# Cross-attention with keys projected instead of queries, raw context attended in row tiles, and inputs laid out by the host

## What is computed

```python
# attention: query = layernorm(x), key = value = ctx (B=32, S=64, D=128), H=8
q = jnp.einsum('bsd,hdk->bhsk', query, Wq)
k = jnp.einsum('btd,hdk->bhtk', key, Wk)
v = jnp.einsum('btd,hdv->bhtv', value, Wv)
A = jnp.einsum('bhsk,bhtk->bhst', q, k)
A = m * A + (1.0 - m) * MASK_VALUE
A = jax.nn.softmax(A, axis=-1)
o = jnp.einsum('bhst,bhtv->bshv', A, v).reshape(...)
x1 = _layernorm(value + o @ Wo, gamma[0], beta[0])
x2 = x + _layernorm(x1 + relu(x1 @ W1 + b1) @ W2 + b2, gamma[1], beta[1])
# experts, on m = layernorm(x2): route to 4 of 16 (groups first), plus 2 shared
out = x2 + sum_e combine[:, e] * ((silu(m @ gate_e) * (m @ up_e)) @ down_e) + shared
```

## Time and profile before

| | |
|---|---|
| time, median of 3 runs | 350.35 us (350.18 to 351.27) |
| profiled execution | 350.7 us, its span 348.3 us |
| busy shares | PE 90%, PEld 73%, DVE 76%, ACT 52%, POOL 48% |
| granted TensorE clock, mean | 0.982 |
| instructions | 5536 |
| first keys or queries matmul | 16.12 us |
| first scores of c = 0, 1, 2, 3 | 23.06, 52.75, 86.36, 121.06 us |

### The profile page before, as it was taken

How to read it: one execution, slowest core, us unless ns; L and a number is a source line. 1 busy time by engine, 2 the same in 40 slices (tenths; PEclk the granted TensorE clock), 3 DMA queues, 4 the chain that set the end, 5 groups by cost and what they waited for, 6 DMA issues and landing times.

```text
span 348.3 us, 5536 instructions
## 1 busy us (share of the span) xinstructions
PE 312.4 (90%) x1683; PEld 254.7 (73%) x1683; DVE 263.7 (76%) x597; ACT 181.5 (52%) x338; POOL 168.9 (48%) x166
## 2 busy tenths in 40 slices
PE   3999899999999998986979799998989898989893
PEld 3979789798979896763858577776767676768662
DVE  2718426947994798898897956968888897969895
ACT  2564663476547653744528245555555645555541
POOL 3006413635563545267743468555655646464530
PEclk9999999999999999998998899999999999999998
DMA  8995000000000000004000065232333332333104
GB/s 240 347 272 191 3 0 3 0 0 2 3 1 0 2 0 2 2 2 128 0 0 1 2 176 194 92 107 104 120 120 120 120 105 89 112 116 120 60 0 122
DMA packets 18775, 26.81 MB, mean 77 GB/s; under 512 B 1330, under 2 KB 13124, under 8 KB 18628
## 3 DMA queue, kind: packets, MB, share of 16 engines
q1 hardware_dynamic: 16676, 25.52, 22.4%
q10 hardware_dynamic: 2080, 1.05, 1.0%
HBM read 25.38 MB, written 1.18 MB: 76 GB/s over the span
## 4 chain that ended last, share of the span: by engine, by line
PE 42%; DVE 22%; issue 15%; ACT 8%; POOL 8%; DMA 1%; DVEq 1%; POOLq 0%; ACTq 0%
PE bank L1223 8%; PE bank L1138 7%; PE bank L1201 7%; PE bank L1140 6%; PE bank L1139 6%; POOL wT L456 6%; DVE wT L1054 5%; DVE wT L1071 3%; ACT wT L682 3%; DVE cen L787 3%; PE bank L1250 2%; PE bank L1280 2%; DVE sc_m L830 1%; ACT prob_T L563 1%; DMA wqk_in<-in_L_xattn_Wq 1%
## 5 line engine op out<-in xcount | busy, mean ns | idle before, releaser
L1138 PE MATMUL bank<-mT_hi,we_hi 128*128 128x512 f32 x128 | 52.2, 408 | 3.1 <-DVE ctx_all L850 1.7
L1140 PE MATMUL bank<-mT_hi,we_lo 128*128 128x512 f32 x128 | 50.8, 397 | 0.0
L1139 PE MATMUL bank<-mT_lo,we_hi 128*128 128x512 f32 x128 | 50.7, 396 | 0.0
L456 POOL TENSOR_TENSOR wT<-wT,wqk_in 128x512 f32<-128x512 f32 x25 | 36.7, 1479 | 22.2 <-DVE wT L1054 18.2
L682 ACT ACTIVATE wT<-bank 128x512 f32<-128x512 f32 x72 | 42.6, 592 | 7.1 <-PE bank L1140 7.0
L693 ACT CAST qk_lo<-wT 128x512 fp32r<-128x512 f32 x36 | 22.3, 620 | 45.5 <-POOL wT L456 21.8
L1054 DVE TENSOR_TENSOR wT<-bank,wT 128x512 f32<-128x512 f32 x64 | 43.4, 679 | 2.2 <-POOL wT L456 2.2
L1061 DVE TENSOR_TENSOR vo_lo<-wT,qk_lo 128x512 fp32r<-128x512 f32 x32 | 32.2, 1006 | 12.6 <-ACT qk_lo L693 11.9
L1061 DVE TENSOR_TENSOR vo_hi<-wT,qk_hi 128x512 fp32r<-128x512 f32 x32 | 32.0, 999 | 10.4 <-ACT qk_hi L693 9.8
L456 POOL TENSOR_TENSOR wT<-wT,wvo_in 128x512 f32<-128x512 f32 x18 | 24.7, 1374 | 26.9 <-DVE wT L1054 26.9
L693 ACT CAST qk_hi<-wT 128x512 fp32r<-128x512 f32 x36 | 22.3, 620 | 26.7 <-POOL wT L456 16.7
(11 more groups left out here) (201 smaller groups left out, 686.1 us busy)
## 6 DMA issues: line engine op xcount, KB each, us to landing
wvo_in<-comb_dram SPq DMA_DIRECT2D x16, 512.0 KB, 3.6
wqk_in<-comb_dram SPq DMA_DIRECT2D x15, 512.0 KB, 3.7
mask_row<-in_mask_BxS_ff SPq DMA_DIRECT2D x1, 1024.0 KB, 9.1
out_x<-ctx_all SPq DMA_DIRECT2D x4, 256.0 KB, 2.9
x_all<-in_x SPq DMA_DIRECT2D x1, 768.0 KB, 8.3
ctx_all<-in_ctx SPq DMA_DIRECT2D x1, 768.0 KB, 10.5
wqk_in<-in_L_xattn_Wq ACTq DMA_DIRECT2D x1, 512.0 KB, 5.0
wqk_in<-in_L_xattn_Wk ACTq DMA_DIRECT2D x1, 512.0 KB, 5.9
```

What stands on the lines that cost most here:

```text
L456: pool.tensor_tensor(act[k % 2], s_u[k % 2], comb[i][:, c * CW:(c + 1) * CW], ALU.mult).then_inc(weighed_ready, 1)
L1138: pe.matmul(dst, w_hi, m_hi, start=start, stop=False)
L1139: pe.matmul(dst, w_hi, m_lo, start=False, stop=False)
L1140: return pe.matmul(dst, w_lo, m_hi, start=False, stop=stop)
```

## The change

The weights arrive laid out so that they need no transposes, and all inputs and the output are arranged by the host such that each partition's part is one run. Keys are projected by the folded weights from the masked context, in the place of the queries; the masked context is made on POOL. The tokens are no longer split. Scores of a tile are two fp32 matmuls of 512 columns (one for each sequence), each with 64 columns of weights, into the two halves of the partitions of one bank. The probabilities attend the raw context: four matmuls over 64 partitions each, for which a second copy of the context with its halves of partitions exchanged is loaded (`ctx_swap`). ACT copies the two results to `o_T`, and `project` multiplies them by Wv Wo head by head, in plain fp32. Values, the split of Wv Wo, and the second copy of `spread` leave. Two work banks are left instead of three; the experts use other banks and buffers, with a third pair of `we_hi`, `we_lo` of its own.

```diff
@@ loads @@
-            sp.dma_start(wv_in, wv.rearrange("h d v -> d h v")).then_inc(ld_wv, 16)
-            sp.dma_start(wo_in, wo.rearrange("(h v) d -> v h d", v=P)).then_inc(ld_wo, 16)
-            sp.dma_start(mask_row[:], mask.rearrange("b s -> (b s)").partition_broadcast(P)).then_inc(ld_mask, 16)
...
+            sp.dma_start(ctx_all[:, 0:TPC, :], ctx_in[:, 0:TPC, :]).then_inc(ld_c0, 16)
+            sp.dma_start(mask_col[:], mask_tok).then_inc(ld_mask_col, 16)
+            sp.dma_start(x_all[:, 0:TPC, :], x[:, 0:TPC, :]).then_inc(ld_x0, 16)
+            for half in range(2):
+                sp.dma_start(w_in[:, 1, half], w_attn[:, 1, half]).then_inc(ld_w[1][half], 16)
+            for r in range(2):
+                rows = slice(r * half_p, (r + 1) * half_p)
+                sp.dma_start(mask_add[rows].rearrange("p t s -> p (t s)"),
+                             mask_pairs[r].partition_broadcast(half_p)).then_inc(ld_mask, 16)
+            for now, ld in ((slice(0, TPC), ld_swap0), (slice(TPC, NT), ld_swap)):
+                for r in range(2):
+                    sp.dma_start(ctx_swap[r * half_p:(r + 1) * half_p, now, :],
+                                 ctx_in[(1 - r) * half_p:(2 - r) * half_p, now, :]).then_inc(ld, 16)
+                if now.start == 0:
+                    sp.dma_start(ctx_all[:, TPC:, :], ctx_in[:, TPC:, :]).then_inc(ld_c, 16)
+                    sp.dma_start(x_all[:, TPC:, :], x[:, TPC:, :]).then_inc(ld_x, 16)
...
+            sp.dma_start(w1_in[:], w1).then_inc(ld_ffn, 16)
+            sp.dma_start(w2_in[:], w2).then_inc(ld_ffn, 16)
+            sp.dma_start(w_exp[:], w_exp_in).then_inc(ld_exp, 16)
@@ POOL @@
+            def mask_context(c):
...
+                now = slice(c * TPC, (c + 1) * TPC)
+                pool.tensor_tensor(ctx_m[:], ctx_all[:, now, :], mask_col[:, now].unsqueeze(2)
+                                   .to_broadcast([P, TPC, P]), ALU.mult).then_inc(ctx_m_ready, 1)
...
                 if last:
                     add_b2(c - 1)
                 if c + 1 < CH:
+                    mask_context(c + 1)
                     inverse_root(0, c + 1)
                 subtract_max(c, 2)
@@ ACT @@
+            def heads_out(c, p):
+                n = c * TPC + p
+                if n >= 2:
+                    a.wait_ge(av_full, n - 1)
                 for j in range(2):
+                    a.wait_ge(o_full[j], n + 1)
+                    a.copy(o_T[p % 2][:, j].rearrange("p h s -> p (h s)"), o_bank[j][:]).then_inc(o_taken[j], 1)
...
-                for s in range(2):
-                    rows = slice(s * SEQ, (s + 1) * SEQ)
-                    last = a.copy(prob_T[p % 2][rows, :, s, :],
-                                  t_bank[rows, :].rearrange("p (h s) -> p h s", s=SEQ))
+                a.copy(prob_T[p % 2][:].rearrange("p h b s -> p (h b s)"), t_bank[:]).then_inc(prob_T_ready, 1)
...
-                value(c, 0)
                 exponent(c, 0)
-                value(c, 1)
                 exponent(c, 1)
...
                 spread(c, 0)
+                if last:
+                    hidden(c - 1, 0)
                 exponent(c, 2)
...
-                value(c, 2)
+                heads_out(c, 0)
                 if last:
                     hidden(c - 1, 1)
                 spread(c, 1)
                 exponent(c, 3)
-                value(c, 3)
+                if c + 1 < CH:
+                    cT_high(c + 1)
+                heads_out(c, 1)
@@ VectorE @@
-                for s in range(2):
-                    last = v.tensor_tensor(
...
+                v.tensor_tensor(sc_m[i][:], sc_bank[:].rearrange("p (h t) -> p h t", t=SEQ),
+                                mask_add[:, n:n + 1, :].to_broadcast([P, NH, SEQ]), ALU.add).then_inc(sc_taken, 1)
...
                 mask_and_max(c, 3)
+                if c + 1 < CH:
+                    cT_low(c + 1)
                 add_ctx(c, 0)
...
             gate_up(0, 0)
+            add_ctx(CH - 1, TPC - 1)
+            v.wait_ge(y_ready, NT)
+            statistics(1, CH - 1, tokens(y, CH - 1))
+            combine(0)
+            gate_up(0, 1)
+            normalise(1, CH - 1, tokens(y, CH - 1))
             take_combine(0)
-            normalise(1, CH - 1, tokens(y, CH - 1))
-            gate_up(0, 1)
@@ TensorE @@
+            def scores(c, p):
+                n = c * TPC + p
...
                 for s in range(2):
                     b = 2 * p + s
-                    for hp in range(HP):
...
+                    pe.matmul(sc_bank[s * SEQ:(s + 1) * SEQ, :], xnT[:, b * SEQ:(b + 1) * SEQ],
+                              k_T[:, b, :, :].rearrange("p h t -> p (h t)"), start=True, stop=True).then_inc(sc_full, 1)
...
             def attend(c, p):
...
+                for s in range(2):
+                    for j in range(2):
+                        rows = slice(j * SEQ, (j + 1) * SEQ)
+                        held = ctx_all if s == j else ctx_swap
+                        last = pe.matmul(o_bank[j][:].rearrange("p (h b s) -> p h b s", b=2, s=SEQ)[:, :, s, :],
+                                         held[rows, n, :], prob_T[p % 2][rows, :, s, :], start=True, stop=True)
...
+            def project(c, p):
...
                 for h in range(NH):
-                    last = pe.matmul(av_bank[:, 0:P], prob_T[p % 2][:, h, :, :].rearrange("p b s -> p (b s)"),
-                                     v_o[p % 2][:, h, :], start=(h == 0), stop=(h == NH - 1))
+                    last = pe.matmul(av_bank[:, 0:P], o_T[p % 2][:, h % 2, h // 2, :], vo[:, h, :],
+                                     start=(h == 0), stop=(h == NH - 1))
...
+                    keys(c, range(0, 2))
                 if last:
                     attend(c - 1, 2)
...
+                    keys(c, range(2, 4))
                 if last:
                     turn_probs(c - 1, 3)
+                    project(c - 1, 2)
...
+                keys(c, range(4, 6))
+                if last:
+                    attend(c - 1, 3)
+                keys(c, range(6, NH))
+                if last:
+                    project(c - 1, 3)
                 if c == 0:
+                    pe.wait_ge(fold_hi, 4)
+                    pe.wait_ge(ld_swap0, 32)
+                    pe.wait_ge(ld_small, 16)
+                    pe.wait_ge(ld_ffn, 32)
...
                 turn_probs(c, 1)
-                values(c, 3)
+                project(c, 0)
                 attend(c, 1)
+                if c + 1 < CH:
+                    turn_ctx(c + 1)
+                if last:
+                    ffn_down(c - 1)
+                project(c, 1)
                 turn_probs(c, 2)
-                if last:
-                    ffn_down(c - 1)
+                if c + 1 < CH:
+                    turn_xn(c + 1)
```

516 lines of the change are left out of this document (207 added, 309 removed).

## The result

The changed kernel took 367.88 us (median of 4 runs, 366.47 to 368.61) against 350.26 (4 runs, 349.71 to 351.27): a ratio of 1.0495, with a 95% interval of 1.0455 to 1.0535. The forecast was 359.5, with a range of 347 to 371. The profiled run of after took 368.1 us, with a span of 366.3; before it was 350.7 and 348.3.

What follows compares the result with a forecast made beforehand. VectorE's list was taken to bound each group's scoring half, TensorE the attending half. From 350.7: groups and handover +9.5, start −3.3, store −0.4, TensorE's clock +3.3 gave 359.8 profiled, 359.5 by the median; range 347 to 371.

Steps and rivals of the forecast that it cites:

- scoring half: First part of a group, first scores to scores 3's end: VectorE gapless, TensorE work nearly free; c = 2 15.3 to 13.1 us.
- c = 2: Middle group of 512 tokens, between its first scores and the next group's: 34.7 to 36.7 us, 2.0 longer.
- attending half: Rest of a group, after scores 3: TensorE hardly idle, its work paid; in c = 2 19.4 to 23.6 us.
- Prices on TensorE: Per tile of 128 tokens: values 1.38 us removed; scores 1.79 to 1.29, attending 1.79 to 1.08; projection adds 1.79.
- by order: Matmul passes in program order, only neighbours in different array parts meeting: scores 3 slots, 1.29 us; attending 5 of 8, 1.08.
- Rival 1: Scores and attending: tile pairs run fully side by side and the clock holds; 349.3 us, 347 to 352; chance 0.13.
- rival 4: Each array shape change costs a drain of 0.16 to 0.26 us: +7 to +11, 367 to 371; chance 0.17.
- c = 0: First group: 29.7 to 32.6 us, +2.9; no FFN work covers the copies; scores 3 end 9.3 after scores 0 begin.
- c = 1: Second group: attending half 4.2 longer, scoring half 14.2 to 12.8 us; +2.8 in all.
- The handover: Last group to last x1: scoring −2.2; tile 1's result 9.7 after scores 3, not 6.9; chain +4.0, net +1.8 us.
- The start: Up to the first scores: weight transposes go, keys begin near 12; first scores at 19.8 against 23.06, −3.3 us.
- Removed at nothing: ScalarE's 0.59 us per tile and VectorE's some 1.7 saved, worth nothing, as neither is late in the attending half.

Runs made afterwards that it cites:

- keys in the pauses: Changed kernel with small loads issued earlier and next group's keys projected in the current group's scoring half: 355.32 us, ratio 1.0169 to the kernel before.
- two heads: Changed kernel with only two of eight heads projected by Wv Wo, the other heads' share left out: 350.9 us.
- the clock held up: Changed kernel with extra split matmuls, results unused, in TensorE's pauses of the scoring half: 366.14 us, ratio 1.0446 to the kernel before.
- the loads ahead: Changed kernel with vector row, router weights, w1 and w2 loaded ahead of the swapped context: 364.92 us, ratio 1.0419 to the kernel before.
- the experiment with the sum: Changed kernel with VectorE's sum of tile 3's exponents ahead of adding tile 1's result in the last group: 367.71 us, ratio 1.0496 to the kernel before.
- the handover experiment: Kernel with keys in the pauses, with the last tile attended, projected and added before the first expert products: 353.32 us, against 355.32.

## Why the prediction was right, and where it was not

*What bounds the kernel.* Right, and the base of all the rest: TensorE idles in the scoring half (3.9 us of waits in c = 2, some 5 forecast) and pays in the attending half. The experiment with keys in the pauses used exactly that and took back 9.6 us; that with two heads shows four fifths of the projections' cost in the time.

*Prices on TensorE.* The chain of waits of after gives one tile's scores, its attending and a projection (start us, us, what):

```profile
98.34 1.06 PE bank L1142 x4
...
112.61 1.06 PE bank L1165 x8
113.68 1.05 PE bank L1198 x2
114.73 0.44 PE bank L1150 x4
115.17 1.79 PE bank L1178 x16
```

The projection is 1.79, as priced; attending 1.06 against my 1.08; scores 1.06 against 1.29. But the ground was wrong, and the price of attending was right by luck. I took 5 of 8 slots, by order; the rows at 112.54 show four full pairs, 0.86, and 0.1 to 0.2 lost at each change of shape (the first slot takes 0.31 to 0.32 instead of 0.215; between split passes of 0.23, from 124.50 to 126.23, an attending group takes 1.73 where the passes alone are 1.32). Rival 1's mechanism (full pairs) and rival 4's (a cost for each change, at the low end of its 0.16 to 0.26 or below) are both borne out, and their sum is near my middle.

The Trainium skill (TensorE: Matmul & The Clock Gate, Part 3) says that matmuls start and end in program order, without reordering. The traces don't bear that out for fp32 matmuls of two passes each: in the kernel after, the first pass of the second matmul starts at 112.55, ahead of the second pass of the first at 112.86, and with the order of the matmuls exchanged the pairs stayed as they were. The Trainium skill (TensorEngine Tiling (Array Packing), Key Properties) states that a change of tiling mode drains TensorE; the rows agree in that such changes cost time, 0.1 to 0.2 us each.

*c = 2.* Scoring half 13.1 forecast, 14.3 measured, 12.9 with the clock held up: the step was right, and the clock's 1.4 there was under-sized (0.8 of the 3.3 us fell to a group); but with the clock held up the whole group was only 0.8 shorter, as the attending half took the rest. The list from mask 0 to mask 2 took 9.82 (99.49 to 109.31), 9.64 forecast. One sentence was wrong, and the prediction had named it among its signs: in that trace scores 3 did not wait for mask 2, which began at 109.31, but for an up-projection at half clock behind the transposed probabilities, which ended at 110.9. The same holds for c = 0 and c = 1; in c = 3 they waited 0.22 for the mask, and with the clock held up 0.33 in c = 1 and c = 2. So at the full clock VectorE's list holds scores 3 back, as forecast; at the low clock TensorE's own list comes as late or later. Attending half 23.6 forecast, 23.0 measured.

*c = 1.* +2.8 forecast and measured. That this agrees to the tenth is luck: in three other traces the group took 1.2 to 1.3 us more, and the forecast had the clock's part on top.

*c = 0.* +2.9 forecast, +5.5 measured. The term that was mis-sized is the clock: TensorE had just stood 4.83 us, and was granted 0.50 from 28 to 40. With the loads ahead the group took 33.8, so 1.4 of the excess of 2.6 went with that stand; the other 1.2 was not taken apart. 1.9 of the 2.6 lie ahead of attending: 11.2 us from scores 0 to the end of scores 3, 9.3 forecast. Project 1 waited 1.70, as priced at 2.0, and project 0 waited 0.40, priced at 0.35.

*The handover.* Adding tile 1's result 9.7 after scores 3 forecast, 9.4 measured (150.1 to 159.46). The failing step is the next, the way from there through statistics to the last x1, which I priced at 1.2 longer: this term of the sum was mis-sized, for want of TensorE's part in it. It took 20.3 us, against 16.0 before (144.44 to 160.42): +4.3. I had followed VectorE's list and left TensorE's out, where transposing probs 3 waits 2.38 (gone in the experiment with the sum, 2.5 of the 4.3), and where projections and two expert products follow (0.8 to 1.0 by the traces of the handover experiment, which start from the kernel with keys in the pauses). The rest was not taken apart.

*The start.* The largest error, 6.9 us. Keys at 12 failed since I let the folds start at 4.5 and run without a break: they started at 5.68, and two of the four halves waited another 0.71 and 0.55 for their loads; keys began at 14.99. First scores at 19.8 failed since I used the best-filled stretches (339 and 370 GB/s): between 11 and 23 us the queues moved 247 and 271 GB/s. By 26.3 us, when the last of w1 and w2 landed, they had moved 7.3 MB at a mean of 278 GB/s, where I had counted 6.2: over 1 MB of the experts' weights, issued behind, came in beside them. The prediction had named loads that hold the first scores to 23 as what would show it wrong.

*Removed at nothing.* ScalarE's and VectorE's savings were priced at nothing and VectorE's 11.4 us are indeed nowhere in the time.

The time lay in the range and on the side named as the likeliest, 8.4 us above the forecast. The errors that made this up (start 6.9, c = 0 2.6, handover 3.1) have one sign, and that the range held them is partly luck: its upper end came from rival 4's +7 to +11 for changes of shape, and loads, clock and handover are what filled it.

## What to carry to other kernels

Before a change that takes work off the busiest engine, write down in which stage that work stood: if it stood under another engine's list, its removal gains nothing, its replacement in a stage where the engine is busy is paid nearly in full (four fifths here), and the pause it leaves can drop TensorE's clock for the work behind it. Order loads by when each is first waited for, and look for what stands *behind* that wait on every engine. When one wait is mended, read the next before counting the gain: here between none of it (the sum in front) and four fifths (the projections) arrived.

## What the runs showed of the hardware

- fp32 matmuls on the two halves of the rows (64 of 128 each), and those on the two halves of the columns, run in pairs, side by side: eight passes of 256 columns, or four of 512, in 1.06 us, where one by one they would be 1.72. For the halves of the rows this held in both orders of the four matmuls. Each change between shapes of the array cost 0.1 to 0.2 us.
- A pause of 2.23 us ahead of a run of matmuls, in a stretch of 4 us with TensorE busy for 2.27, was followed by a granted clock of 0.67 over 4 us; with the pause shortened and filled with unused matmuls (busy for 3.51) it stayed at 1.00. In the scoring halves, stretches of 4 us with 1.49 and 1.79 busy were followed by 4 us at 0.50, one with 1.98 by 0.72; where unused matmuls made it 3.76, the clock stayed at 1.00.
- Where in the scoring half the low clock sets in differs between executions: the scores of tile 3 in c = 1 took 1.37 in the trace of the kernel after and 1.98 in that of the kernel with the sum in front, whose instructions are the same up to there.
